# A decoder with a recurrent router: norms started on three of four batches, scores moved ahead of a value half, ranks by 9 products, input products in batch order with three tiles inside the pipeline

## The reference

```
x = x + attn(ln(x)); x = x + xattn(ln(x), ctx); x = x + ffn(ln(x))     # layers 0 to 3
```

```
h0 = hidden.mean(axis=1) @ ctx_w.T + ctx_b          # 8 x 1024
xw = hidden @ gru_w_ih.T                            # 800 x 3072
def step(h, xw_t):                                  # 100 steps
    hw = h @ gru_w_hh.T                             # 1024 -> 3072
    r, z = sigmoid(xr + hr), sigmoid(xz + hz)
    n = tanh(xn + r * hnn)
    return (1 - z) * n + z * h
expr = hidden @ expr_w.T                            # 800 x 1024
scores = (1 - cos(expr, h)) * (1 + penalty); top 2 of 8; gated experts, plus a shared one
```

## Time and profile before

| | us |
|---|---|
| three timed runs | 3233.26, 3235.72, 3252.05 |
| median | 3235.72 |
| the profiled execution | 3258.05 |
| its span | 3256.2 |
| TensorE busy | 2996.5 (92%) |
| VectorE busy | 1549.5 (48%) |
| ScalarE busy | 743.9 (23%) |
| GpSimd busy | 236.6 (7%) |
| granted clock, mean | 0.945 |

### The profile page before, as it was taken

The page is one execution under the profiler, slowest core; times in us unless marked ns, Lnnn a source line. Parts: engine busy times, 40 slices in busy tenths (PEclk is TensorE's granted clock), DMA queues, the critical chain, the costliest instruction groups (busy, mean ns, idle before and its releaser), DMA issues.

```text
span 3256.2 us, 63316 instructions
## 1 busy us (share of the span) xinstructions
PE 2996.5 (92%) x25733; PEld 1697.8 (52%) x25733; DVE 1549.5 (48%) x4080; ACT 743.9 (23%) x1830; POOL 236.6 (7%) x433
## 2 busy tenths in 40 slices
PE   6888889889988999999889989999999999999897
PEld 4554456669755555555546643444444444444387
DVE  4645345411146566300564521466666666666643
ACT  2331133211122445211014411111111111111111
POOL 2001101020210000000200000000000000000011
PEclk8989989799988999999889979999999999999999
DMA  4000000258430000411000057000000000000176
GB/s 146 1 1 1 12 23 2 87 192 327 173 117 1 1 1 1 140 52 65 1 1 1 2 137 224 13 19 25 23 21 23 22 24 25 19 26 22 39 263 222
DMA packets 80720, 202.96 MB, mean 62 GB/s; under 512 B 32254, under 2 KB 55467, under 8 KB 67844
## 3 DMA queue, kind: packets, MB, share of 16 engines
q1 hardware_dynamic: 76568, 192.75, 18.0%
q0 software_dynamic: 3968, 7.56, 0.7%
HBM read 170.06 MB, written 37.53 MB: 64 GB/s over the span
## 4 chain that ended last, share of the span: by engine, by line
PE 81%; DVE 9%; DMA 4%; ACT 3%; issue 2%; POOL 1%; SPq 1%; another core or an unknown queue 0%; DVEq 0%; POOLq 0%; ACTq 0%
PE banks L1216 31%; PE banks L1036 9%; PE banks L868 4%; PE banks L588 4%; PE banks L762 3%; PE banks L541 3%; PE banks L1184 2%; PE banks L1101 2%; PE banks L1113 2%; PE banks L890 2%; PE banks L908 1%; PE banks L1263 1%; PE banks L914 1%; PE banks L930 1%; PE banks L657 1%
## 5 line engine op out<-in xcount | busy, mean ns | idle before, releaser
L1216 PE MATMUL banks<-arena 128*32 128x384 f32 x12800 | 1034.3, 486 | 1.9 <-DVE arena L2185 1.1
L1216 PEld LDWEIGHTS banks<-arena 128*32 128x32 f32 x12800 | 416.6, 110 | 613.7 <-issue 609.1
L1592 ACT ACTIVATE arena<-arena 128x256 f32<-128x256 f32 x200 | 83.4, 417 | 759.0 <-DVE arena L2197 759.0
L2197 DVE TENSOR_TENSOR arena<-banks,arena 128x256 f32<-128x256 f32 x200 | 84.9, 425 | 199.4 <-PE banks L1216 198.3
L1036 PE MATMUL banks<-arena 128*128 128x400 f32 x512 | 172.5, 499 | 1.5 <-DVE arena L2147 0.8
L868 PE MATMUL banks<-arena 128*100 128x256 f32 x512 | 151.7, 455 | 17.6 <-ACT arena L1517 5.3
L1327 ACT ACTIVATE arena<-banks 128x512 f32<-128x512 f32 (+2 forms) x120 | 68.5, 572 | 415.1 <-PE banks L1101 154.9
L588 PE MATMUL banks<-XNT,arena 128*128 128x400 f32 x384 | 151.2, 536 | 8.3 <-ACT XNT L1338 3.9
L762 PEld LDWEIGHTS banks<-arena 32*121 32x121 f32 x1536 | 105.7, 196 | 62.3 <-ACT arena L1436 47.3
L1036 PEld LDWEIGHTS banks<-arena 128*128 128x128 f32 x512 | 97.1, 190 | 76.8 <-DVE arena L2147 1.4
L1790 DVE TENSOR_REDUCE arena<-banks 100x4 f32<-100x1444 f32 x64 | 106.3, 1661 | 63.6 <-PE banks L718 63.5
(11 more groups left out here) (378 smaller groups left out, 4211.7 us busy)
## 6 DMA issues: line engine op xcount, KB each, us to landing
arena<-fc SPq DMA_DIRECT2D x22, 1024.0 KB, 4.7
arena<-pj SPq DMA_DIRECT2D x22, 1024.0 KB, 6.3
arena<-gu SPq DMA_DIRECT2D x21, 1024.0 KB
arena<-whh SPq DMA_DIRECT2D x32, 384.0 KB, 17.3
arena<-dn SPq DMA_DIRECT2D x21, 512.0 KB, 5.7
arena<-xw SPq DMA_DIRECT2D x400, 24.0 KB
xw<-arena SPq DMA_DIRECT2D x6, 1536.0 KB, 15.5
arena<-hh SPq DMA_DIRECT2D x16, 512.0 KB, 3.3
```

The source lines that it names most:

```text
L1216: last = nc.tensor.matmul(banks[32 * j:32 * j + 32, 2 * c + i, 0:384].rearrange("p (g n) -> p g n", g=3), hT[:, 1 - i, 32 * ub:32 * ub + 3 ...
L1592: nc.scalar.activation(rz[:, c, :], pre[:, c, :], ACT.Sigmoid).then_inc(sem["rz_done"], 1)
L2197: nc.vector.tensor_tensor(pre[:, c, :].rearrange("p (g n) -> p g n", g=2), banks[:, 2 * c + i, 0:2 * P].rearrange("p (g n) -> p g n", g=2) ...
```

## The change

1. `norm_group` works in two parts. VectorE raises `known` once after the third batch of a group (three small operations on three columns) and once after the fourth; GpSimd takes its 12 small operations and three normalisations, then 12 more and the fourth.
2. In pipeline A, where the next item is of kind "first", `score_round` stands between `key_rows` and the second `weighted_half`.
3. `chosen` has a ninth, empty batch; the ranks and totals come from 9 products.
4. Tokens are in the order (batch, position) in XNT, `xw` and `shown`. The 8 rows of a step are 100 rows apart, and the expressions of a lap are ten transfers of 8 rows, issued in steps 4 to 7 of the lap.
5. Tiles 0 to 2 (18 units of two matmuls) are made inside pipeline C. The store of tiles 0 and 1, `ctx_w` (into the place of `whh` block 4, which is loaded last) and `whh` block 5 stand ahead of the wait for the pipeline's end.

```diff
+        def stored(i):
+            return 16 * (i // 2 + 1)
+        def drain_units(i, r):
+            return {(15, r): range(2 * r, 2 * r + 2), (16, 0): range(8, 11), (16, 1): range(11, 14), (16, 2): range(14, 16), (16, 3): range(16, 18)
+                    }.get((i, r), ())
+        DRAINED = 3
...
+            def drain_unit(m):
+                i, q = m // 6, m % 6
+                u, full_ = open_m("C", "xw", i, q)
+                for kk in range(C):
+                    last = nc.tensor.matmul(u[:, :], XNT[:, kk, i * P:i * P + P], wih_flat[:, kk, 512 * q:512 * q + 512], start=kk == 0, stop=kk == C - 1)
+                last.then_inc(sem[full_], 1)
...
                             key_rows(ph, i, r)
+                        if then == "first" and r == 0:
+                            score_round(ph, i + 1, 0)
                         if past == "first" and r == 0:
                             weighted_half(ph, i - 1, 1)
-                        if then not in (None, "mixture", "wide") and (r == 0 or then == "cross"):
+                        if then not in (None, "first", "mixture", "wide") and (r == 0 or then == "cross"):
                             score_round(ph, i + 1, r)
...
                             key_rows(ph, i, 0)
+                        units = list(drain_units(i, r)) if ph == "C" else []
+                        if units[:1] == [0]:
+                            wait("l_gru", 16)
+                            need(ph, "xT", len(KINDS[ph]), 0, 1)
                         if now == "cross":
                             key_rows(ph, i, 2 * r)
+                            if units:
+                                drain_unit(units.pop(0))
                         if later == "cross":
...
                             key_rows(ph, i, 2 * r + 1)
+                        if now == "cross" and units:
+                            drain_unit(units.pop(0))
                         if now == "mixture":
...
-                nc.tensor.matmul(u[0:S, 0:B * E], earlier, chosen.rearrange("p b e -> p (b e)"), start=True, stop=False, skip_group_check=True)
-                for b in range(B - 1):
-                    later = u[0:S, (b + 1) * E:B * E].rearrange("p (b e) -> p b e", e=E)
-                    nc.tensor.matmul(later, ones[0:S, 0:S], chosen[:, b, :].unsqueeze(1).to_broadcast([S, B - 1 - b, E]),
-                                     start=False, stop=b == B - 2, skip_group_check=True)
+                nc.tensor.matmul(u[0:S, 0:(B + 1) * E], earlier, chosen.rearrange("p b e -> p (b e)"), start=True, stop=False,
+                                 skip_group_check=True)
...
-                    last = nc.tensor.matmul(u[0:S, B * E:B * E + E], ones[0:S, 0:S], chosen[:, b, :], start=b == 0, stop=b == B - 1,
-                                            skip_group_check=True)
+                    later = u[0:S, (b + 1) * E:(B + 1) * E].rearrange("p (b e) -> p b e", e=E)
+                    last = nc.tensor.matmul(later, ones[0:S, 0:S], chosen[:, b, :].unsqueeze(1).to_broadcast([S, B - b, E]),
+                                            start=False, stop=b == B - 1, skip_group_check=True)
...
-            pe.wait_ge(sem["l_gru"], 16)
-            input_gates(0)
+            input_gates(DRAINED)
...
-                        dst = XNT[:, kk, 0:4 * S].rearrange("p (b s) -> p b s", b=4)
-                        if ph == "C":
-                            dst = XNT[:, kk, :].rearrange("p (s b) -> p b s", b=B)[:, 0:4, :]
-                        nc.scalar.activation(dst, u[:, 0:4 * S].rearrange("p (b s) -> p b s", b=4), ACT.Copy).then_inc(sem[evac_], 1)
+                        nc.scalar.activation(XNT[:, kk, 0:4 * S], u[:, 0:4 * S], ACT.Copy).then_inc(sem[evac_], 1)
+            def drain_unit(m):
+                i, q = m // 6, m % 6
+                if m == 12:
+                    act.wait_ge(sem["xw0"], stored(0))
+                evacuate(xw_out[:, i % 2, 512 * q:512 * q + 512], P, 512, "C", "xw", i, q)
...
+                        for m in drain_units(i, r) if ph == "C" else ():
+                            if m >= 11:
+                                drain_unit(m)
...
-                if b % 4 == 3:
-                    x, y = stats[:, b - 3:b + 1, 7], rstd[:, b - 3:b + 1]
+                if b % 4 >= 2:
+                    some = slice(b - 2, b + 1) if b % 4 == 2 else slice(b, b + 1)
+                    x, y = stats[:, some, 7], rstd[:, some]
...
+                        units = [m for m in drain_units(i, r) if m < 11] if ph == "C" else []
+                        if (i, r) == (15, 1):
+                            for m in units:
+                                drain_unit(m)
+                            units = []
...
-                pool.wait_ge(sem["known"], norms_before(ph, s, g) + 1)
-                four = slice(4 * g, 4 * g + 4)
-                x, y, t = stats[:, four, 7], rstd[:, four], rstd[:, B + 4 * g:B + 4 * g + 4]
-                for _ in range(3):
-                    step(nc.gpsimd.tensor_tensor(t, y, y, ALU.mult))
-                    step(nc.gpsimd.tensor_tensor(t, t, x, ALU.mult))
-                    step(nc.gpsimd.tensor_scalar(t, t, -0.5, 1.5, ALU.mult, ALU.add))
-                    step(nc.gpsimd.tensor_tensor(y, y, t, ALU.mult))
-                for b in range(4 * g, 4 * g + 4):
-                    last = nc.gpsimd.tensor_scalar(XN[:, b * D:(b + 1) * D], X[:, b * D:(b + 1) * D], stats[:, b, 6:7],
-                                                   rstd[:, b:b + 1], ALU.subtract, ALU.mult)
+                for part, (lo, hi) in enumerate(((4 * g, 4 * g + 3), (4 * g + 3, 4 * g + 4))):
+                    pool.wait_ge(sem["known"], 2 * norms_before(ph, s, g) + part + 1)
+                    x, y, t = stats[:, lo:hi, 7], rstd[:, lo:hi], rstd[:, B + lo:B + hi]
+                    for _ in range(3):
+                        step(nc.gpsimd.tensor_tensor(t, y, y, ALU.mult))
+                        step(nc.gpsimd.tensor_tensor(t, t, x, ALU.mult))
+                        step(nc.gpsimd.tensor_scalar(t, t, -0.5, 1.5, ALU.mult, ALU.add))
+                        step(nc.gpsimd.tensor_tensor(y, y, t, ALU.mult))
+                    for b in range(lo, hi):
+                        last = nc.gpsimd.tensor_scalar(XN[:, b * D:(b + 1) * D], X[:, b * D:(b + 1) * D], stats[:, b, 6:7],
+                                                       rstd[:, b:b + 1], ALU.subtract, ALU.mult)
...
+            def store_tile(i):
+                to, width = (xw, 3 * G) if i < TILES else (shown, G)
+                at_ = i % TILES * P
+                rows = min(P, T - at_)
+                sp.dma_start(to[at_:at_ + rows, :], xw_out[0:rows, i % 2, 0:width]).then_inc(sem["xw%d" % (i % 2)], 16)
+            for key in (("C", 0, 1, "q", 3, 1), ("C", 1, 1, "q", 3)):
+                _, full_, _, value = unit_of(key)
+                sp.wait_ge(sem[full_], value)
+            load(cw.rearrange("p k g -> p (k g)"), "ctx_w", "l_cw")
+            load_whh([(j, early_whh // 4, early_whh % 4) for j in range(4)])
+            def store_drained(i):
+                for q in (4, 5):
+                    _, _, evac_, value = unit_of(("C", "xw", i, q))
+                    sp.wait_ge(sem[evac_], value)
+                store_tile(i)
+            for i in range(2):
+                store_drained(i)
+            sp.wait_ge(sem["phase"], 4)
+            load(cb[0:1, :], "ctx_b", "l_cw")
...
-            x_rows = xw.rearrange("(s b) (j g u) -> s j b g u", b=B, j=4, g=3)
-            def load_x(row, i):
+            x_rows = [xw[2 * k:T + 2 * k].rearrange("(b s) (j g u) -> s j b g u", b=B, j=4, g=3) for k in range(2)]
+            def load_x(row, i, ahead=0):
...
-                    src_ = x_rows[bass.ds(row, 1), j].rearrange("o b g u -> (o b) g u")
+                    src_ = x_rows[ahead][bass.ds(row, 1), j].rearrange("o b g u -> (o b) g u")
...
-            expr_rows = shown.rearrange("(c p) g -> c p g", p=ROWS)
+            expr_rows = shown.rearrange("(b c t) g -> c t b g", b=B, t=LAP)
+            def load_expressions(lap, some):
+                for t in some:
+                    sp.dma_start(expr[B * t:B * t + B], expr_rows[lap, t].rearrange("o b g -> (o b) g")).then_inc(sem["l_expr"], 16)
...
-            for i in range(2 * TILES):
-                rows = min(P, T - i % TILES * P)
-                later = i - TILES + 1
-                sp.wait_ge(sem["a_evac"], MARK["xw"]["a_evac"] + (3 * i + 3 if later <= 0 else 3 * TILES + later))
-                sp.wait_ge(sem["d_evac"], MARK["xw"]["d_evac"] + (3 * i + 3 if later <= 0 else 3 * TILES + later) + (i > 0))
-                if later <= 0:
-                    sp.dma_start(xw[i * P:i * P + rows, :], xw_out[0:rows, i % 2, :]).then_inc(sem["xw%d" % (i % 2)], 16)
-                    load_whh(parts[8 + 4 * i:12 + 4 * i])
-                else:
-                    at_ = (i - TILES) * P
```

(28 more changed lines are left out.)

66 lines of the change are left out of this document (35 added, 31 removed).

## The result

| | before | changed |
|---|---|---|
| timed runs | 22 | 22 |
| median, us | 3238.61 | 3224.84 |
| lowest to highest, us | 3233.26 to 3262.11 | 3207.24 to 3247.47 |
| ratio, 95% interval | | 0.9955 [0.9936, 0.9973] |
| span of the profiled execution, us | 3256.2 | 3242.3 |

The kernel became 14 us faster, in the direction of the forecast, but by 0.4 of its size: 35.4 us were forecast. Two later comparisons of the same two kernels gave 0.9929 [0.9898, 0.9960] and 0.9925 [0.9899, 0.9950], some 24 us. All three are short of 0.989. One execution of the kernel before, 3944.8 us at a mean clock of 0.732, is left out of every comparison.

The account below looks back on a forecast made before the run. It took the input stage to be bound by bytes in one DMA queue, with recurrence work on TensorE unchanged. −23.7 − 8.8 − 1.6 − 1.3 = −35.4 us gave 3200 us from the 3235.7 median, range 3190 to 3210.

Parts of the forecast that it names:

- Input stage: Between third pipeline and recurrence: earlier transfers and tiles start the recurrence at 2003.5 instead of 2027.2, −23.7 us.
- The second rival: At the third pipeline's end: clock stays 0.71 then 0.50 under the drained units, sum only −7 us, 3228; chance 0.10.
- The third rival: In the input stage: TensorE, not the DMA queue, sets the end; start 10 us earlier, 3190 us; chance 0.08.
- Ranks: Rank products on TensorE: the eight totals over the batches go, nine wider products remain, −1.3 us.
- Norms: TensorE's four waits for normalised X: three batches start before the fourth's statistics, shortening the waits, −8.8 us.
- Scores: Next scores on TensorE ahead of the second value half: work fills a wait, key rows come sooner, −1.6 us.
- The sum: Whole kernel: −35.4 us, from 3258.05 profiled to 3222.7, and from the 3235.7 median to 3200 us.
- Slower: Rival in the recurrence: rows 100 apart delay 98 steps by 1 us each, 3298 us; chance 0.03.

Follow-up runs that it names:

- more_bytes: Changed kernel with four w_hh pieces (1536 KB) loaded a second time behind the store of tile 3; last turn to recurrence 91.4 us, mostly 82.8 to 83.3 otherwise.
- before_again: The kernel before, unchanged, run for a second profile; ratio to before 0.9996.
- three_alone: The kernel before with only the norms in two parts, scores ahead of the second value half and ranks by 9 products; ratio to before 0.9984.
- norms_alone: The kernel before with only the norms in two parts; ratio to before 0.9982.
- the filled kernels: Useless TensorE products put in waits: changed kernel 0.9878 and 0.9895 of before, kernel before 0.9965, changed kernel with norms in one part 0.9894.
- drain_alone: The changed kernel with its norms, scores and ranks parts undone; ratio to before 0.9936.
- norms_undone: The changed kernel with the norms in one part again; ratio to before 0.9902.

## Why the prediction was wrong, step by step

- **Input stage, −23.7.** Right: −21.9 in the first pair of profiles, −24.2 between the means of five and eight. (The terms as printed, 1989.7 and 10.4, 2 and 1 us, give 2003.1 and not 2003.5.) Inside it one step was off: the store of tile 1 was to begin at 1908.5 and was issued at 1919.87, 1912.0 when shifted as below; the end came out right within 2 us all the same. The store that was last to bind landed before 1999.01; shifted by item 15's later start, 7.9 us, that is 1991, and the forecast had 1989.7. The second rival (the clock stays at 0.50 under the drained units) is wrong: 1.00 in 1890 to 1910. The Trainium skill, "TensorE: Matmul & The Clock Gate", Part 1, says that the clock follows how busy the engine has been, and in that stretch the trace agrees: busy for 20.00 of 20 us. The third rival (the queue does not bind) is wrong by `more_bytes`.
- **Ranks, −1.3.** Right: from the first rank product to the product behind them 2.77 us in before_again (644.06 to 646.83), 1.53 in three_alone. That is TensorE's time there; no run has this part alone.
- **Norms, −8.8.** The step that failed. The waits changed as worked out, to 0.2 us. What failed was to book a shorter wait at its length, with the clock behind it put down as unchanged. With the shorter wait the clock fell to 0.50 in the products behind in five of six profiles, +8.9 us in three stretches: +3.3 us over the waits and the stretches where −5.1 was booked. Where the clock was kept, in norms_alone and the filled kernels, the gain was 4 to 7 us. The timed runs show no gain of the norms that is clear of noise, alone or inside the changed kernel. The prediction took the clock from one row at one place and asked it only for the drained units; it asked nothing of the clock behind the waits that it shortened. Why the fall comes more often with the shorter wait, if it does, stays open.
- **Scores, −1.6.** Open. The stretch that holds them, from the turn at 12 us to the one at 168, takes 155.0 to 158.8 us in the five profiles without the change (mean 157.0) and 153.2 to 157.1 in the nine with it (mean 154.9). That is the forecast's direction and size, but either group spreads over 4 us. No experiment had this part alone.
- **The sum.** It was carried from a profiled execution with a mean clock of 0.945 to a median. That execution took 8.5 us more in the three stretches behind the turn at 417 than three other profiles with the norms in one part. And the changed kernel's own profile was again one at 0.945: 20 us of its distance to the forecast's 3222.7 are the third pipeline's fall. Its two other profiles, 3215.5 and 3211.2 us, lie under the forecast.
- **Slower.** No sign: the recurrence's steps are equal to 0.1 us in the sum, with its rows 100 rows apart.

In the two later comparisons, −23 and −24 us, some 12 of the forecast's 35.4 are missing. The norms' 8.8 are most of that by the profiles; the timed runs agree with it and are too few to prove it. The first comparison misses 9 us more, because the kernel before was faster in it (mean 3242.9 us, later 3250.8 to 3255.3). Whether that was its clock or another cause is not shown: the clocks of those runs are not on record.

## What to carry to other kernels

In a kernel that waits in many small pieces, a wait need not be worth its length: ask what the clock does behind it, and count a shortened wait only when the stretch behind it is shorter too. Compare two profiles of the same kernel before a stretch of one is explained, and read each timed run with its mean clock. Where a wait can't be removed, useless products into the bank that is overwritten next are a cheap thing to try (here −11 us on the kernel before).

## What the runs showed of the hardware that was not expected

- A kernel of identical instructions takes 153.4 or 174.5 us in one part, with the granted clock mostly at 1.00 (mean 0.96) or down to 0.61 and 0.76 over 20 us (mean 0.84). Idle time hardly tells them apart: TensorE has 11.2 us of it in the execution that took 174.5 us, 10.8 and 10.5 in the two that took 153.5, and 11.2 in `more_bytes`, which took 153.6 us. What differs is where the clock's last fall stood ahead of the turn at 1684. Among the eight profiles with the norms in two parts it stood 6.4 to 6.5 us ahead in four, and three of these took 169.7 us or more; it stood 5.1 to 5.9 us ahead in the other four, and each of these took 153.6 us or less.
- The values are few. From the turn at 1684 to the next one fourteen profiles of ten kernels took 67.3 to 67.6 us (three), 69.4 to 69.7 (five), 71.7, 75.5 (two) or 82.4 to 82.5 (three), and from there to the last but one 83.9 to 84.0 (seven), 87.2, 88.8 (four) or 92.0 (two). `before_again` and `drain_alone`, with the same instructions on TensorE up to there, agree within 0.1 us in four stretches (261.65 and 261.56, 61.69 and 61.71, 75.48 and 75.46, 88.81 and 88.80), while the kernel before in its first profile had 71.66 and 83.95 for the last two.
- Four of the fourteen profiles (before, norms_alone, norms_undone, more_bytes) have one wait of VectorE of 8.7 to 8.8 us that the profile puts down to no semaphore of the program (in before from 673.56), during the routed experts; TensorE waits 3.0 to 3.6 us there. What it is stays open:

```profile
682.33 0.75 DVE L2073 TENSOR_TENSOR X<-X,banks 100x256 f32<-100x256 f32 x2 [8.77 <-remote]
```
